# Graph attention with one-hot matmuls: comparison and weighing operands moved from SBUF to PSUM, exponentials written twice

## What is computed

```python
edge_index = jnp.stack([src, dst])
x = x + gnn(_layernorm(x), edge_index, W, att_src, att_dst, bias)
x = x + ffn(_layernorm(x)[None], mask, wr, br, w1, b1, w2, b2)[0]

# gnn, N = 12500, 4 heads of 64 channels, a self loop added to each node
xp = (x @ W).reshape(n, H, C)
alpha = leaky_relu(a_src[src] + a_dst[dst], 0.2)
ex = exp(alpha - amax[dst])
w = ex / segment_sum(ex, dst)[dst]
out = elu(segment_sum(xp[src] * w[..., None], dst).reshape(n, H * C) + bias)

# ffn: of all nodes those with the largest x @ wr get gelu(x @ w1 + b1) @ w2 + b2, times x @ wr
```

## Time and profile before

| | |
|---|---|
| median of 3 runs | 2780.69 us |
| lowest and highest run | 2779.0 and 2808.06 us |
| span of the profiled execution | 2587.4 us |
| POOL busy | 1878.6 us (73%) |
| PE busy, PE weight loads | 1983.9 us (77%), 1692.1 us (65%) |
| DVE busy, ACT busy | 1625.5 us (63%), 946.1 us (37%) |
| granted TensorE clock, mean | 0.877 |
| GpSimd's gathers L608, 1613 of them | 1835.2 us busy, mean 1138 ns |

### The profile page before, as it was taken

One profiled execution on the slowest core, in us unless ns is written; L12 is line 12 of the kernel. 1 busy time (PEld: TensorE's weight loads), 2 busy tenths in 40 slices (PEclk: granted clock), 3 DMA queues, 4 the chain that ended last, 5 costly groups with the idle time before them and its releaser, 6 DMA issues.

```text
span 2587.4 us, 44011 instructions
## 1 busy us (share of the span) xinstructions
PE 1983.9 (77%) x10893; PEld 1692.1 (65%) x10894; DVE 1625.5 (63%) x3934; ACT 946.1 (37%) x1960; POOL 1878.6 (73%) x1686
## 2 busy tenths in 40 slices
PE   6936787787788778877877887787778778877862
PEld 5835676666677667666766676666667667666752
DVE  5745656666666666656666666666666566666667
ACT  3512333333343333334333433434343343334330
POOL 2257777777777777777777777777777777777730
PEclk9968888898889889888998988898898899898886
DMA  7544454454455445444544544454445445444548
GB/s 251 174 122 120 133 140 123 135 140 125 134 140 138 124 134 139 135 124 136 140 125 136 140 136 123 135 138 134 124 138 140 121 135 140 134 124 136 150 135 302
DMA packets 245118, 365.39 MB, mean 141 GB/s; under 512 B 91173, under 2 KB 180417, under 8 KB 245090
## 3 DMA queue, kind: packets, MB, share of 16 engines
q0 software_dynamic: 77488, 214.85, 31.3%
q1 hardware_dynamic: 138002, 121.74, 15.3%
q10 hardware_dynamic: 29600, 28.49, 3.3%
HBM read 326.04 MB, written 38.89 MB: 141 GB/s over the span
## 4 chain that ended last, share of the span: by engine, by line
POOL 30%; PE 28%; DMA 12%; issue 11%; DVE 11%; SPq 3%; DVEq 1%; ACTq 1%; ACT 1%; POOLq 1%
POOL rows L608 30%; PE ag_ps L914 14%; DMA rows<-node_rows,srci 7%; DMA dsti<-in_dst 5%; PE h_ps L893 5%; PE y_ps L903 4%; PE ag_ps L820 3%; DVE oh L1160 3%; DVE base L1376 1%; DVEq L365 1%; SPq L365 1%; SPq L433 1%; PE tr_ps L882 1%; ACTq L771 1%; DVE rows L1192 1%
## 5 line engine op out<-in xcount | busy, mean ns | idle before, releaser
L608 POOL DMA_INDIRECT rows<-node_rows,srci x1613 | 1835.2, 1138 | 491.3 <-issue 463.6
L914 PE MATMUL ag_ps<-rows,oh 128*128 128x260 f32 x3322 | 769.0, 389 | 69.0 <-DVE rows L1192 68.8
L914 PEld LDWEIGHTS ag_ps<-rows,oh 128*128 128x128 f32 x3322 | 624.1, 192 | 189.6 <-DVE rows L1192 72.6
L903 PE MATMUL y_ps<-w2s,hT 128*128 128x256 f32 x1568 | 530.4, 499 | 7.6 <-ACT hT L709 7.6
L1192 DVE TENSOR_TENSOR rows<-rows 128x768 f32<-128x768 f32 (+2 forms) x685 | 498.9, 800 | 31.7 <-ACT rows L726 31.7
L903 PEld LDWEIGHTS y_ps<-w2s,hT 128*128 128x128 f32 x1568 | 384.8, 258 | 73.6 <-issue 7.7
L893 PEld LDWEIGHTS h_ps<-xnT,w1s 128*128 128x128 f32 x3136 | 398.9, 210 | 22.3 <-issue 18.4
L893 PE MATMUL h_ps<-xnT,w1s 128*128 128x128 f32 x3136 | 401.2, 291 | 0.5 <-ACT xnT L699 0.5
L882 PE MATMUL tr_ps<-ident,steps_of_rows 128*128 128x128 f32 x196 | 63.8, 426 | 427.1 <-DVE steps_of_rows L1263 427.1
L882 PEld LDWEIGHTS tr_ps<-ident,steps_of_rows 128*128 128x128 f32 x196 | 26.9, 193 | 465.6 <-DVE steps_of_rows L1263 465.6
L1175 DVE TENSOR_TENSOR zz<-rows,edge_dm 128x68 f32<-128x68 f32 x98 | 22.5, 229 | 455.4 <-DMA rows<-node_rows,srci 453.0
(11 more groups left out here) (169 smaller groups left out, 1504.8 us busy)
## 6 DMA issues: line engine op xcount, KB each, us to landing
dbc<-dst SPq DMA_DIRECT2D x97, 544.0 KB
rows<-node_rows,srci POOLq DMA_INDIRECT x1613, 2.8
selfr<-node_rows SPq DMA_DIRECT2D x98, 130.0 KB
base<-in_x SPq DMA_DIRECT2D x14, 896.0 KB, 5.0
base<-in_x SPq DMA_DIRECT2D x98, 128.0 KB
ffn_rows<-yb ACTq DMA_DIRECT2D x96, 128.0 KB
node_rows<-base SPq DMA_DIRECT2D x13, 910.0 KB, 5.8
out<-base SPq DMA_DIRECT2D x3, 1024.0 KB, 4.3
```

The costliest lines, as they stand in the source:

```text
L608: pool.indirect_dma_start(out=rows[:, b, t, :], out_offset=None, in_=table, in_offset=bass.IndirectOffsetOnAxis(ap=srci[:, b, t:t + 1], ax ...
L903: nc.tensor.matmul(y_ps[:, 0:D], hT[:, m, :], w2s[:, m, :], start=(m == 0), stop=False)
L914: nc.tensor.matmul(ag_ps[b][:, 0:ROW], oh[:, b, t, :], rows[:, b, t, :], start=(t == 0), stop=False).then_inc(tile_done, 1)
```

## The change

The numbers 0 to 127 are copied once into the last 128 columns of `xl_ps`, and the one-hot comparison reads them from there. ScalarE computes the window's exponentials twice from the same `diff`: first into 68 unused columns of `lk_ps` (`ex_ps`), and then into the rows as before. The weighing multiplies read them from `ex_ps`. VectorE waits for the first copy (`ex_ok`), TensorE for the second (`exr_ok`) before a window's first product. Of both kinds of VectorE instruction one input then lies in SBUF and one in PSUM, where both lay in SBUF; the output is in SBUF as before. The order of each queue stays as it is; the only instructions added are one copy of 128 columns before the first window and one activation of 68 columns in each window.

```diff
@@ tensors
         tr2 = [t[:, 0:D].rearrange("p (c q) -> p c q", c=DC) for t in (tr_ps, xl_ps)]
+        iota_ps = xl_ps[:, 512 - P:512]
+        ex_ps = lk_ps[:, TILES * VK:TILES * (VK + H)].rearrange("p (t h) -> p t h", h=H)
+        assert TILES * (VK + H) <= 512
@@ ScalarE, exponentials
                 act.wait_ge(diff_ok, w + 1)
-                nc.scalar.activation(rows[:, b, 0:tiles_of(w), D:ROW], diff[:, 0:tiles_of(w), :], ACT.Exp).then_inc(ex_ok, 1)
+                nc.scalar.activation(ex_ps[:, 0:tiles_of(w), :], diff[:, 0:tiles_of(w), :], ACT.Exp).then_inc(ex_ok, 1)
+                nc.scalar.activation(rows[:, b, 0:tiles_of(w), D:ROW], diff[:, 0:tiles_of(w), :], ACT.Exp).then_inc(exr_ok, 1)
@@ TensorE, window
                     pe.wait_ge(zn_ok, w - 1)
+                pe.wait_ge(exr_ok, w + 1)
                 for t in range(tiles_of(w)):
@@ VectorE, one_hots
-                nc.vector.tensor_tensor(oh[:, b, 0:n, :], iota_d[:, :].unsqueeze(1).broadcast_to([P, n, P]),
+                nc.vector.tensor_tensor(oh[:, b, 0:n, :], iota_ps.unsqueeze(1).broadcast_to([P, n, P]),
                                         dloc[:, 0:n].unsqueeze(2).broadcast_to([P, n, P]), ALU.is_equal).then_inc(oh_ok, 1)
@@ VectorE, weigh
                     v = rows[:, b, a:a + m, 0:D].rearrange("p t (h c) -> p t h c", h=H)
-                    e = rows[:, b, a:a + m, D:ROW].unsqueeze(3).broadcast_to([P, m, H, C])
+                    e = ex_ps[:, a:a + m, :].unsqueeze(3).broadcast_to([P, m, H, C])
                     nc.vector.tensor_tensor(v, v, e, ALU.mult).then_inc(scaled, 1)
@@ VectorE, before the first window
+            then(nc.vector.tensor_copy(iota_ps, iota_d[:, :]))
             one_hots_turned(0, 0, 0)
```

More of the change, by code:

```diff
@@ L297, in build @@
             sem2(n) for n in ("ld_src", "ld_dst", "ld_dbc", "ld_self", "ld_x", "gath", "gath_last", "y_st"))
-        (oht_ok, loc_ok, oh_ok, lk_ok, dm_ok, zs_ok, zm_ok, zl_ok, diff_ok, ex_ok, scaled, tile_done, agg_ok, selfx_ok,
+        (oht_ok, loc_ok, oh_ok, lk_ok, dm_ok, zs_ok, zm_ok, zl_ok, diff_ok, ex_ok, exr_ok, scaled, tile_done, agg_ok, selfx_ok,
          self_ok, rden_ok, zn_ok, zb_ok, zmin_ok, zexp_ok, xa_ok, x1_ok, st_ok, mv_ok, ln_ok, rs0_ok, ve_ok, sq_ok,
          half_ok, rstd_ok, xn_ok, base_ok, wcol_ok, wt_ok, tr_ok, xnT_ok, h_ok, hT_ok, y_ok, yb_ok) = sems(
-            "oht_ok loc_ok oh_ok lk_ok dm_ok zs_ok zm_ok zl_ok diff_ok ex_ok scaled tile_done agg_ok selfx_ok "
+            "oht_ok loc_ok oh_ok lk_ok dm_ok zs_ok zm_ok zl_ok diff_ok ex_ok exr_ok scaled tile_done agg_ok selfx_ok "
             "self_ok rden_ok zn_ok zb_ok zmin_ok zexp_ok xa_ok x1_ok st_ok mv_ok ln_ok rs0_ok ve_ok sq_ok "
```

## The result

The changed kernel took 3534.94 us (median of 4 runs, 3534.22 to 3537.47) beside 2784.94 us of the kernel before (4 runs, 2779.0 to 2808.06): ratio 1.265, interval 1.259 to 1.271, 26% slower. In three later sessions the same two kernels gave 2308.33 against 2580.5, 2305.86 against 2583.54 and 2306.18 against 2587.46 us: ratios 0.894 (0.892 to 0.896), 0.893 (0.891 to 0.894) and 0.892 (0.886 to 0.898), 11% faster. Both are real: **the machine was in one of two conditions for a whole session**, *disturbed* (the kernel before takes 2779 to 2834 us) or *quiet* (2577 to 2590 us). The condition's cause isn't known. The forecast, 2671 us, is that of neither.

A forecast was written before the change was run, and what follows sets the result against it. GpSimd's gathers set the pace, 23.74 us per window; after the change a TensorE-VectorE ring of 22.63 would. 96 x (23.74 - 22.63), with the first two windows 110 us, off 2780.69 gives 2671 us; range 2620 to 2790.

The forecast's parts named there:

- The holds: Gathers held by VectorE's comparison and weighing multiplies: one PSUM input frees them, taking 187 and 78.5 us off GpSimd.
- VectorE's durations: With one input from PSUM the comparison stays at 2.42 us and the seven weighing multiplies at 5.10; cost 0.
- The ring of 22.63 us: TensorE and VectorE waiting on each other every window: 8.05 + 14.75 - 0.17 us, the pace after the change.
- the sum: Whole-run gain: 96 windows x (23.74 - 22.63) = 107 us, 110 with the first two windows; span 2477 us.
- VectorE's own round: VectorE's work per window, from one `rden` to the next: 18.9 us, fitting within 22.63.
- rival 2: GpSimd's full gain: TensorE's clock returns earlier, pace falls to GpSimd's 21.0 us per window, 2516 us; chance 0.05 below 2620.
- TensorE's chain beside the gathers: From the end of `xn` through turning and half of L903 to the hidden layer's end: 7.26 us, GpSimd running ahead.
- both waits go: Late products, or `rden` late behind loads issued after gathers land, vanish with GpSimd 1.6 us per window ahead.
- The time outside the trace: 193.3 us of run time around the span of 2587.4 us, kept unchanged in the forecast of 2671 us.
- Rival 3: Broadcast PSUM input costs VectorE one cycle more per element: comparison 2.24 us longer, 2889 us; chance 0.12 for over 1% slower.
- waits that I have not seen: Unspecified waits making the kernel over 1% slower: chance 0.02, part of the 0.12 for any slower result.

The follow-up runs named there:

- the paused kernel: The changed kernel with one GpSimd instruction of 1.56 us before each window's ninth gather: 2459.32 us, ratio 0.951 to the kernel before.
- the one with two exponentials: Both exponentials written, the rows' first, with comparison and weighing reading SBUF as in the kernel before: 2802.68 us, ratio 0.999 to that kernel.

## Why the prediction was wrong

1. **The holds (right).** Gathers' mean "near 0.97 us": 966 ns disturbed, 962 quiet. The 195 quiet gathers that fall into a comparison and the 388 that fall into weighing multiplies have a mean excess under 0.001 us, also with the PSUM input as the second operand. Removed were 283.1 us for 265.5 (comparison 198.6 for 187, weighing 84.5 for 78.5). Most of the surplus is luck: the addition of `xn` to `base` (L1265), which the change leaves alone, held 95 gathers for 16.2 us in all before, and at the new pace 7 gathers fall into it, with no excess. The Trainium skill (SBUF — State Buffer, Who interferes with whom) says that a VectorE instruction with at most one SBUF input, outside its two-port modes, doesn't contend with GpSimd; these runs agree, for multiply, comparison and `tensor_reduce`. That section's remark that `tensor_tensor` was not seen to stall such DMAs doesn't hold for these gathers: 3.00 us for 0.95. Its reason, that descriptor generation needs only the write interface, isn't tested by that: the same section has two SBUF inputs contend with what GpSimd reads from SBUF, a gather reads its row numbers `srci` there, and no run separates the two.

2. **VectorE's durations (right).** Comparison 2425 ns for 2425 at 2176 elements, pieces of 256 columns 420 ns for 425, of 768 columns 945 for 953. The Trainium skill (VectorE: DVE Perf Modes, The TRN2 errata) gives a PSUM source some 65 ns more of fixed cost than SBUF; these pairs, in which one of the two inputs moved to PSUM, show none of it.

3. **The ring of 22.63 us (wrong, the step that fails in the quiet condition).** The text says that "the self loop's end frees `rden` at 1006.92: 8.05 us". It does not. `residual` works on the window before, and waits for `agg_ok` of that window:

```python
residual(w - 1, i - 1 + b, 1 - b)      # in VectorE's window(w)
dve.wait_ge(agg_ok, w + 1)             # in residual(w)
```

So the self loop that it needs is a whole period old, and the products that had just ended next to `rden` in the earlier trace rows only stood there. The 1.11 us before the first `rden` of the earlier trace rows read "issue": there the sequencer loads the two table entries of `for_extra`. The 1.25 us before the second are put down to TensorE, as in 77 of the 98 gaps of that trace; but these gaps are 1.17 us in the mean and those of "issue" 1.07, so there is hardly a wait in them. A releaser is inferred from an update of the same semaphore in the gap, and here the update is one that the instruction doesn't need. The quiet trace of the changed kernel has `rden` ahead of that self loop:

```profile
716.99 0.18 DVE L1234 RECIPROCAL rden<-ag_ps 128x4 f32<-128x4 f32 x1 [1.15 <-issue]
...
720.35 2.42 DVE L1165 TENSOR_TENSOR oh<-xl_ps,dloc 128x2176 f32<-128x2176 f32 x1
...
721.13 0.95 POOL L611 DMA_INDIRECT rows<-node_rows,srci  x1 [0.30 <-issue]
...
723.32 0.41 DVE L1268 TENSOR_SCALAR steps_of_rows<-base,mv,rstd 128x256 f32 x1
...
725.15 0.58 DVE L1176 TENSOR_REDUCE edge_dm<-lk_ps 128x136 f32<-128x408 f32 x1 [0.34 <-issue]
...
727.62 0.23 DVE L1180 TENSOR_TENSOR zz<-rows,edge_dm 128x68 f32<-128x68 f32 x1 [1.89 <-DMA rows<-node_rows,srci]
...
728.94 5.07 DVE L1197 TENSOR_TENSOR rows<-rows,lk_ps 128x256 f32<-128x256 f32 x7 [0.30 <-ACT lk_ps L729]
...
738.21 0.18 DVE L1234 RECIPROCAL rden<-ag_ps 128x4 f32<-128x4 f32 x1 [1.11 <-issue]
...
739.88 0.60 PE L930 MATMUL ag_ps<-selfr,ident 128*128 128x260 f32 x2
```

`rden` starts at 738.21, the self loop of the newer window at 739.88. In 73 of 96 windows the nearest self loop ends after the start of `rden`, so `rden` can't have waited for it (the median over all 96 is 1.1 us later); in the trace of before in 15, since there VectorE waited 453 us for rows and TensorE had caught up. Without this wait the ring of the sum does not close. VectorE's own round is here 738.21 - 716.99 - 1.89 = 19.33 us without the wait for rows, which the prediction had as 18.9, and TensorE is busy for 18.6 us of each of the two windows below. Both lie below GpSimd's 20.85, so nothing stops GpSimd's gain. Which of them would come next isn't shown. The prediction's rival 2 came true in this condition, with the wrong reason given for it and 0.05 to its name. The prediction's own test was there: "if it stays 0.30 everywhere, GpSimd is still the bound and the ring is shorter than I think".

The clock plays along but doesn't decide. Two windows of the changed kernel, quiet (us; busy us and count of PE, PEld, DVE, ACT and POOL; granted clock, DMA share, GB/s):

```profile
717.00:738.21 21.21, 17.71 (x98) 15.38 (x97) 15.06 (x35) 9.19 (x19) 16.03 (x18) 0.84 0.53 152
738.21:759.50 21.29, 19.50 (x130) 17.21 (x129) 16.13 (x38) 9.16 (x19) 16.11 (x18) 1.00 0.54 147
```

One has part of its stretch at 1.2 GHz and the other none, and both take 21.2 to 21.3 us. TensorE's idle time before the turning fell from 427.1 to 278.7 us, and its mean clock rose from 0.877 to 0.908.

4. **TensorE's chain beside the gathers (wrong, the step that fails in the first result).** The ring has 7.26 us from the end of `xn` to the hidden layer's end, lets GpSimd run ahead and says that "both waits go". In the disturbed window shown this stretch is 25.60 us (1409.22 to 1434.82). Of it 18.47 us pass until the copy of the turned `xn`, which comes only when the run of gathers has ended, 0.50 from the copy's start to the hidden layer, and the hidden layer takes 6.63 us for 3.74: TensorE had stood idle for 14.28 us, and the mean granted clock of its 6.63 us is 0.55. Then GpSimd waits for TensorE, 1228.5 us in all, where the prediction had it wait for nothing that counts. The overlap of gathers and TensorE's chain, which the sum took for granted, isn't there, and 33.68 us stand where it had 22.63. Why TensorE's signals are late beside gathers stays open.

5. **The time outside the trace (wrong, and why no row warned of step 4).** "With the 193.3 us around it, the median 2671." All runs here lie 1.7 to 1.8 us above their spans, so the term of 193.3 us stands for no time around the program but for the other condition. The trace didn't show what the runs were bound by: no row has the wait that decided. Quiet, the forecast's method would have said a span of 2587 - 110 = 2477 us; measured were times of 2306 to 2308, 280 us below and not 110.

6. **The rivals.** Rival 3, the slower one, had the sign of the first result but not its mechanism: no instruction of VectorE grew. What came belongs to the 0.02 that it kept for "waits that I have not seen"; nothing in the list was an effect of gathers on other engines' queues.

## What to carry to other kernels

Before a span is used, subtract it from the time of its runs: in every run here 1.7 to 1.8 us were left, and the 193 us of the prediction meant that the trace was of another condition than the times, so that no sum made on it could predict them. Before two engines are joined into a ring, read in the kernel which iteration's semaphore the wait names; that one ended beside the other in the trace proves nothing, nor does the releaser that the profile infers. And run the old kernel beside every new one: without its 2587 us the 2459 us of the paused kernel would have passed for a cure of 3535.

## What the hardware showed unexpectedly

- The same kernel takes 2306 us or 3535 us, its predecessor 2585 or 2780 to 2834, by session. Chip number 4 appeared with both conditions, numbers 13, 14 and 15 with the quiet one.
- In the disturbed condition, beside an unbroken stream of GpSimd's indirect DMAs, 109 of SyncE's 740 DMA issues take about 0.70 us for 0.33, and in the first windows TensorE's matmuls start multiples of 0.70 us apart. The packets of the gathers' queue take no longer in all than in the quiet condition: 23.1% of 3532.5 us is 816 us, and 35.4% of 2306.8 us is 817.
- What costs time in one condition protects in the other: the comparison that holds one gather for 3.0 us costs 199 us of GpSimd's time when quiet, and its absence costs 727 us when disturbed (3536.3 - 2809.73).
- The version to keep depends on the condition: quiet, the changed kernel is the fastest of all that ran; disturbed, the kernel before and the one with two exponentials, which are equal.
